# The order of one head's step, written anew on all five engines around row sums that run as column tiles of the TensorE array

## The reference, cut to what matters

```
q, k, v = silu(conv4(x @ W.T))                 # per head 128 wide, causal, 4 taps
q = scale**2 * rms(q); k = scale * rms(k)      # needs sum(q*q), sum(k*k) over the head
g = -exp(A_log) * softplus(x @ Wfa.T @ Wfb.T + dt_bias)
beta = sigmoid(x @ Wb.T)
for each token t:                              # S is 128 x 128 per batch and head
    S = S * exp(g_t)
    S = S + k_t * (beta_t * (v_t - k_t @ S))
    o_t = q_t @ S
out = rms(o) * o_norm_w * sigmoid(gate)
x = x + out @ Wo.T
x = x + experts(layernorm(x))
```

## Time and profile before

| what | value |
|---|---|
| median of 3 runs | 5112.28 us (5112.07 to 5114.02) |
| the profiled execution's own time | 5110.11 us |
| its span, first to last instruction | 5108.4 us |
| granted TensorE clock, mean | 0.988 |
| busy: PE / DVE / ACT / POOL | 93% / 73% / 66% / 56% |
| attention part, about | 0 to 4300 us |
| expert part, about | 4300 to 5108 us |

### The profile page before, as it was taken

One profiled execution on the slowest core, in us unless ns is written; L12 is line 12 of the kernel. 1 busy time (PEld: TensorE's weight loads), 2 busy tenths in 40 slices (PEclk: granted clock), 3 DMA queues, 4 the chain that ended last, 5 costly groups with the idle time before them and its releaser, 6 DMA issues.

```text
span 5108.4 us, 111671 instructions
## 1 busy us (share of the span) xinstructions
PE 4746.5 (93%) x28928; PEld 3617.8 (71%) x28928; DVE 3750.8 (73%) x8897; ACT 3347.4 (66%) x7216; POOL 2884.6 (56%) x6210
## 2 busy tenths in 40 slices
PE   6999999999999999999999999999999997999999
PEld 3777777777777777777777777777777775555555
DVE  5878777777777777777787777777777773555555
ACT  5777777777777777777777777777777772111111
POOL 4766666666666666666666666767676671000000
PEclk8999999999999999999999999999999998999999
DMA  2211111111111111111111111111111111000000
GB/s 82 62 36 37 37 37 37 33 36 35 37 35 36 37 37 37 32 37 35 37 35 37 37 37 37 37 33 37 35 37 35 37 28 35 13 8 12 8 12 13
DMA packets 214012, 173.09 MB, mean 34 GB/s; under 512 B 146272, under 2 KB 163936, under 8 KB 213216
## 3 DMA queue, kind: packets, MB, share of 16 engines
q1 hardware_dynamic: 213344, 165.49, 11.4%
HBM read 119.03 MB, written 46.40 MB: 32 GB/s over the span
## 4 chain that ended last, share of the span: by engine, by line
PE 64%; ACT 19%; issue 11%; POOL 2%; DVE 2%; DMA 1%; ACTq 0%; POOLq 0%; SPq 0%; DVEq 0%
PE bank L1589 10%; PE bank L1380 9%; PE bank L1281 8%; PE bank L1428 5%; PE bank L1402 4%; PE bank L1358 4%; PE bank L1599 4%; ACT L638 3%; ACT lx L574 3%; PE bank L1333 2%; PE bank L1433 2%; PE bank L1289 2%; PE bank L1415 2%; ACT T L584 2%; ACT e_sb L634 2%
## 5 line engine op out<-in xcount | busy, mean ns | idle before, releaser
L1380 PE MATMUL bank<-kq,kl 128*128 128x128 f32 x6144 | 853.3, 282 | 47.5 <-DVE kq L879 39.9
L387 POOL TENSOR_TENSOR kl<-kl,tot 128x256 f32<-128x256 f32 x768 | 507.1, 660 | 588.5 <-PE bank L1380 588.4
L1380 PEld LDWEIGHTS bank<-kq,kl 128*128 128x128 f32 x6144 | 750.0, 191 | 108.0 <-issue 70.1
L1281 PE MATMUL bank<-xT,par 128*128 128x512 f32 x1536 | 760.4, 605 | 0.4 <-ACT bexp L531 0.4
L406 POOL TENSOR_TENSOR mul<-pm,rm 32x14 f32<-32x14 f32 (+6 forms) x1792 | 528.4, 295 | 123.4 <-issue 23.0
L410 POOL TENSOR_TENSOR rm<-rm,mul 32x14 f32<-32x14 f32 (+6 forms) x1792 | 511.8, 286 | 142.3 <-POOL mul L406 2.4
L879 DVE TENSOR_TENSOR kq<-kq,tot 128x512 f32<-128x512 f32 x768 | 536.6, 699 | 0.0
L889 DVE COPY_PREDICATED AT<-mask,bank 128x256 f32<-128x256 uint32 x896 | 468.3, 523 | 0.0
L367 POOL TENSOR_TENSOR rstd<-rstd,minus_half 128x4 f32<-128x4 f32 x32 | 32.2, 1007 | 737.6 <-DVE rstd L824 737.6
L797 ACT ACTIVATE q<-bank 128x512 f32<-128x512 f32 x144 | 86.1, 598 | 521.4 <-PE bank L1589 521.4
L1402 PE MATMUL bank<-T,lx 128*128 128x64 f32 x3072 | 386.3, 269 | 3.8 <-issue 3.8
(11 more groups left out here) (176 smaller groups left out, 12512.9 us busy)
## 6 DMA issues: line engine op xcount, KB each, us to landing
par<-params_dram SPq DMA_DIRECT2D x128, 519.0 KB, 3.4
blocks_out<-lx SPq DMA_DIRECT2D x128, 256.0 KB, 2.0
lx<-blocks_in SPq DMA_DIRECT2D x128, 256.0 KB, 2.7
pm<-blocks_out SPq DMA_DIRECT2D x512, 8.0 KB
blocks_in<-rm SPq DMA_DIRECT2D x512, 8.0 KB
out_dram<-xall SPq DMA_DIRECT2D x16, 512.0 KB, 2.9
xall<-x_dram SPq DMA_DIRECT2D x5, 1536.0 KB, 7.1
lx<-ffn_dram SPq DMA_DIRECT2D x1, 3456.0 KB, 10.8
```

Of the source, the lines that this page charges most:

```text
L387: pool.tensor_tensor(halves(kl[:, :], w)[:, :, 0, :], src, totr.broadcast_to([P, SEQ // (2 * w), w]), ALU.mult).then_inc(s["kl_ready"], 1)
L1281: ins = pe.matmul(bank[t][:, :], par[p][:, at:at + P], chunk(xT, kt, SEQ), start=kt == 0, stop=kt == KT - 1)
L1380: ins = pe.matmul(dst[:, :, n], chunk(left, n), right[:, :, n, :, 1, :], start=True, stop=True)
```

## The change

Only the lists of calls at the end of each `step` are changed; the functions, the waits within them, the buffers and the arithmetic stay. Every engine has the same calls in a step as before. The whole diff, with 16 columns of indentation and the empty lines left out:

```diff
@@ -296,8 +296,6 @@
     sp.wait_ge(s["low_in"], 16 * NCH * (iB + 1))
     sp.sem_inc(s["sp_go"], 1)
-if B:
-    next_params()
 if D:
     blocks_from_pool()
     diagonals_back()
@@ -305,6 +303,8 @@
     low_levels_out()
     blocks_to_pool()
 next_x()
+if B:
+    next_params()
 supersteps(sp, lambda bn, first: None, step)
 sp.wait_ge(s["x_mm"], HIGH * NHEAD)
@@ -458,10 +458,10 @@
 if D:
     eliminate(iD, 10)
+    eliminate(iD, 11)
 if B:
     kl_update(0)
 if D:
-    eliminate(iD, 11)
     eliminate(iD, 12)
     eliminate(iD, 13)
     eliminate(iD, 14)
@@ -473,18 +473,13 @@
     softplus_high()
 if B:
     kl_update(3)
+    kl_update(4)
 if A:
     totals(1)
     totals(2)
     totals(3)
     totals(4)
-if B:
-    kl_update(4)
-if A:
     totals(5)
-    totals(6)
-    totals(7)
-next_rstd()
 if B:
     kl_update(5)
 if C:
@@ -496,11 +491,19 @@
 if B:
     eliminate(iB, 1)
     eliminate(iB, 2)
+if A:
+    totals(6)
+if B:
+    eliminate(iB, 3)
     kl_update(6)
-    eliminate(iB, 3)
+next_rstd()
+if B:
     eliminate(iB, 4)
     eliminate(iB, 5)
     eliminate(iB, 6)
+if A:
+    totals(7)
+if B:
     eliminate(iB, 7)
     eliminate(iB, 8)
     eliminate(iB, 9)
@@ -707,62 +710,64 @@
     after(act, s["su_mm"], 3 * (i - LAG + 1))
     act.activation(kT[pB][:, :], b_x[:, 0:3 * P], ACT.Copy).then_inc(s["kt_ev"], 1)
+if C:
+    w_evict(0)
+if A:
+    tap0(0, "q_mm")
 if B:
     k_copy()
-if C:
-    w_evict(0)
-if A:
-    tap0(0, "q_mm")
+if A:
+    tap0(1, "k_mm")
 if C:
     w_evict(1)
 if A:
-    tap0(1, "k_mm")
     softplus_exp()
     softplus_max()
     softplus_ln()
+if C:
+    w_evict(2)
+if A:
     tap0(2, "v_mm")
-if C:
-    w_evict(2)
 if D:
     t16_scale()
-if B:
-    lt16_scale()
-if A:
-    decay()
 if N:
     turned_x(nb, 0)
+if B:
+    lt16_scale()
 if D:
     tt16_evict()
-if C:
-    w_evict(3)
-if D:
     x_evict(4)
 if N:
     turned_x(nb, 1)
+if C:
+    w_evict(3)
+if A:
+    decay()
+if N:
+    fa_evict(nb)
+if C:
+    output_squares()
 if A:
     silu(0)
     silu(1)
-if C:
-    output_squares()
-if N:
-    fa_evict(nb)
 if D:
     tt_evict(4)
     x_evict(5)
 if A:
     silu(2)
     square(0)
+if B:
+    turned_v()
+if A:
+    square(1)
 if N:
     ga_evict(nb)
-if B:
-    turned_v()
-if A:
-    square(1)
 if D:
     tt_evict(5)
+if C:
+    turned_og()
+if D:
     x_evict(6)
-if C:
-    turned_og()
 if A:
     gate()
 if N:
@@ -1022,85 +1027,85 @@
     l_evict(0)
     kq_update(0)
     qk_evict(0)
+if A:
+    conv(0, 1)
 if C:
     s_update(0)
 if A:
-    conv(0, 1)
+    conv(0, 2)
 if C:
     residual(1)
 if A:
-    conv(0, 2)
     conv(0, 3)
+    conv(1, 1)
 if B:
     l_evict(1)
     qk_evict(1)
-if A:
-    conv(1, 1)
 if C:
     s_update(1)
 if B:
     kq_update(1)
 if A:
     softplus_one()
+if C:
+    residual(2)
+if A:
     softplus_rest()
 if B:
     l_evict(2)
-if C:
-    residual(2)
-if B:
+    qk_evict(2)
     kq_update(2)
-    qk_evict(2)
 if A:
     conv(1, 2)
     conv(1, 3)
 if B:
     l_evict(3)
+    qk_evict(3)
 if C:
     s_update(2)
 if B:
-    qk_evict(3)
+    kq_update(3)
+if C:
+    residual(3)
 if A:
     conv(2, 1)
-if B:
-    kq_update(3)
-if C:
-    residual(3)
-next_moments()
+    conv(2, 2)
+    conv(2, 3)
 if B:
     l_evict(4)
     qk_evict(4)
     kq_update(4)
-if A:
-    conv(2, 2)
 if D:
     t_update(4)
+if B:
+    l_evict(5)
+if C:
+    output_moments()
+if B:
+    kq_update(5)
 if A:
     kq_init(1)
-    conv(2, 3)
-if B:
-    l_evict(5)
-if C:
-    output_moments()
-if B:
-    kq_update(5)
+if B:
     qk_evict(5)
+if C:
+    outputs()
 if D:
     t_update(5)
-if C:
-    outputs()
 if B:
     l_evict(6)
+next_moments()
+if B:
     kq_update(6)
 if A:
     kq_init(0)
 next_scale()
-if D:
-    t_update(6)
 if B:
     qk_evict(6)
 if C:
     residual_stream(0)
     residual_stream(1)
+if D:
+    t_update(6)
 if A:
     scales()
     diagonal()
@@ -1468,26 +1473,26 @@
     pe.matmul(b_s[:, P:2 * P], chunk(TT[pB], n), R if n else chunk(vs[pB], 0),
               start=True, stop=True).then_inc(s["z_mm"], 1)
+if B:
+    level(0)
 if C:
     solve(0)
-if B:
-    level(0)
 if A:
     project(0, 0)
     project(0, 1)
+    project(1, 0)
 if C:
     state_update(0)
 if A:
-    project(1, 0)
+    project(1, 1)
 if C:
     k_times_s(1)
+if B:
+    level(1)
+if C:
     chunk_outputs(0)
-if B:
-    level(1)
-if C:
     solve(1)
 if A:
-    project(1, 1)
     project_f()
 if C:
     state_update(1)
@@ -1497,66 +1502,69 @@
     level(2)
 if A:
     project(2, 0)
+if C:
+    solve(2)
+if A:
     project(2, 1)
-if C:
-    solve(2)
 if B:
     level(3)
 if C:
     state_update(2)
+if N:
+    turn_next_x(nb, 0)
 if A:
     project_g(0)
     project_g(1)
     project_g(2)
-    project_g(3)
-if C:
+if C:
+    chunk_outputs(2)
     k_times_s(3)
 if D:
+    turn_16()
     lt_times_t(4)
 if N:
-    turn_next_x(nb, 0)
-if D:
-    turn_16()
+    turn_next_x(nb, 1)
+if C:
+    solve(3)
 if B:
     level(4)
-if C:
-    chunk_outputs(2)
-    solve(3)
 if N:
-    turn_next_x(nb, 1)
+    next_fa(nb)
 if C:
     state_update(3)
     chunk_outputs(3)
 if D:
     t_products(4)
-if N:
-    next_fa(nb)
 if B:
     level(5)
 if D:
     turn_t(4)
     lt_times_t(5)
+if A:
+    project_g(3)
+if B:
+    turn_v()
 if N:
     next_ga(nb)
 if D:
     t_products(5)
 if B:
-    turn_v()
     level(6)
 if D:
     turn_t(5)
+if C:
+    turn_og()
+if D:
     lt_times_t(6)
-if C:
-    turn_og()
 if N:
     next_beta(nb)
 if A:
     sums()
-if D:
-    t_products(6)
 if C:
     project_out(0)
     project_out(1)
+if D:
+    t_products(6)
 if A:
     turn_sums()
 if B:
```

32 lines of the change are left out of this document (16 added, 16 removed).

## The result

The changed kernel takes 5069.98 us (median of 4 runs, 5069.19 to 5071.58), the kernel before, run beside it on the same chip, 5113.15 us. The ratio is 0.9916, 95% interval [0.9901, 0.9931]: 43 us faster, where 85 were forecast. The profiled execution took 5070.19 us with a span of 5068.5 us.

A forecast was written before the change was run, and what follows sets the result against it. A ring through PE, DVE and a nearly full ACT bounds each step. Terms of -0.71, +0.05 and -0.02 give -0.68 us, times 125 is -85 us: 5027 us, forecast range 5000 to 5050, 8 in 10 within 4975 to 5095.

The forecast's parts named there:

- The ring: Step's chain: PE's first calls, q's convolution, project_f, ACT to square of k, sums, next step; other waits closed give only its gain.
- The ACT term: ACT, softplus to square of k: PE about 1.1 us sooner, so both idle gaps close, 0.71 us a step.
- rival C: POOL takes the bound: elimination steps stretched by DVE, 0.80 us each; one gives 5112 us, two 5215; chance 0.11.
- The start: DVE, step's start: s_update(0) behind q's first conv delays q's last taps some 0.2 us, mostly covered; 0.05 us charged.
- The step's sum: Ordinary step: all terms together -0.68 us, 31.6 to 30.9.
- small overlaps on ACT: ACT within the step: a further gain of 0.02 us a step.
- The POOL term: POOL, step's start: kl_update(0) written 4.9 us into the step, level(1) needs it at about 5.0; room 0.1 us.
- SP at nothing: SP's queue: next_params goes from first call to last, with 5 us of room left; costs nothing.
- The N and loop steps at -0.7: Head 7's step with extra matmuls and the step behind the loop's branch: each taken to gain 0.7 us.
- Rival B: Half the gain: unseen 0.1 to 0.2 us waits at level(1), turn_16 and level(5); 0.34 us a step, 5070; chance 0.20.
- Rival A: More comes back: PE's whole 1.1 us at level(5) reaches the step's end, 4975 us; chance 0.10.

The follow-up runs named there:

- 3: Changed kernel with s_update(0) put back ahead of the first tap of q on DVE, residual(1) behind that tap; 5118.1 us, ratio 1.0019.
- 5: Changed kernel with POOL's totals(1) held until level 4's eviction of kq, totals(4) to (6) moved down among the elimination's steps; 5042.11 us.
- 9: Changed kernel with totals(1) held back, later totals spread, kl_update(0) first on POOL, and the step's start on PE and DVE put back; 4979.19 us.
- 12: Changed kernel with POOL's totals(1) held until level 4's eviction on DVE is done, nothing else moved; 5084.54 us, ratio 0.9961.
- 11: Changed kernel with only the step's start put back as before on PE and DVE (state_update(0), s_update(0), residual(1)); 5055.59 us, ratio 0.9894.
- 4: Changed kernel with kl_update(0) as POOL's first call, ahead of elimination steps 10 and 11; 5064.75 us, ratio 0.9905.
- 10: Changed kernel with next_params put back at the front of SP's queue; 5076.45 us, ratio 0.9942.

## Why the prediction was half right

*The ring* held. In 3 some 0.5 us ahead of `project_f` became 0.5 us a step, in 5 and 9 what was taken out of it came off the step.

*The ACT term, "0.25 and 0.46 both close: 0.71 us a step", is the step that failed.* The mechanism was right and the size wrong: softplus to square went from 19.47 to 18.98 on average, 0.49 instead of 0.71. The premise was "PE reaches `turn_t(4)` and `lt_times_t(5)` about 1.1 us sooner". Counted from the softplus, it reaches them 0.5 us sooner: `level(5)`, right in front of them, starts 12.61 us behind the softplus before and 12.09 in the changed kernel. In 5, without the stretch, it is 11.65, and that is 0.96 sooner, near the 1.1. I had written that `level(5)` then waits for DVE, and took the middle of 0.8 and 1.4 without asking how long DVE's update would last at its new place. It lasts 1.12 us and not 0.69, since POOL's `totals(1)` begins 0.04 us ahead of it. In 5 and 12 the stretch is gone and so is the gap. I had used this very contention, but only for POOL's elimination, as rival C; the same pair of rows had to be asked in the other direction too. The Trainium skill ("SBUF — State Buffer", section "Who interferes with whom") says that a DVE instruction with two SBUF inputs contends with a GpSimd instruction that reads SBUF. The trace agrees (0.69, 1.12, and 0.68 with the neighbour held back); the prediction had quoted it and not applied it here.

With the stretch gone the term is even larger than forecast, 19.47 to 18.56 or 0.9 us. The bracket of 0.29 ahead of `x_evict(5)` cost more than it shows: between the starts of the two evictions lie 0.67 us with it and 0.33 without it [2407.52 to 2408.19, and 2413.72 to 2414.05 in 9], so 0.34.

*The start, "I charge 0.05 us to the ring".* First and last piece went from 12.08 to 12.21 in the mean, +0.13, and putting `s_update(0)` and `state_update(0)` back gave 0.22 in the changed kernel, so the rest of the new start gained 0.1. The path was another one than I had named. I had let the last tap of q eat up 0.23 us of room ahead of `project_f`. But in 3, where `project_f` does wait for that tap, it starts 0.05 us behind its end, so the room was 0.18 in the step that I read and 0.02 in the next one, where `project_f` started 0.07 behind. And in the changed kernel `project_f` starts some 0.24 us behind the last tap in most steps: the tap doesn't bind it. What is late is `level(1)`, 5.10 or 5.24 us behind `level(0)`, against 5.01 in 11. It stands behind `k_times_s(1)`, which reads `s_update(0)`; and that is late by `project(1, 0)`, now ahead of `state_update(0)` on PE, as well as by DVE's order. In the changed kernel 0.5 us of idle stand ahead of the first convolution, so DVE isn't short of time there, only in the wrong order.

*The step's sum.* -0.49 + 0.13 is -0.36, which is what heads 1 to 4 measured. Forecast was -0.68. Of the 0.32 between them the ACT term has 0.22, the start 0.08, and 0.02 were the "small overlaps on ACT", of which nothing is seen. Head 0's step, behind the N step, gained 0.72: its first and last piece had been 12.45 us and is 12.27 now, nearly like the others'. In the kernel before, DVE made the next batch's beta in that step (0.28 and 0.36 us, L840 and L842) ahead of `s_update(0)`, and PE waited for it:

```profile
2384.42 0.49 PE L1457 MATMUL bank<-lx,kq 128*128 128x128 f32 x2 [0.15 <-DVE lx L924]
```

`level(1)` started 4.57 us behind `level(0)` there and 4.15 in the other steps. In the changed kernel it is 5.25, as in the steps of heads 2 and 4: the idle time that now lies ahead of the first convolution takes these 0.6 us in. I had counted head 0's step as an ordinary one.

*The POOL term, "room of 0.1 us", and rival C.* `level(1)` has its kl in time in seven steps of eight. In head 6's it waits 0.26 us, and 4 shows the price, 0.48 us in that step, some 7 us in all. So C was true in one step of eight. It wasn't an elimination that was stretched but `next_rstd`, which my walk had left out, and `inverse_norms`, by 0.38 and 0.44 us, of which I had allowed for neither.

*SP at nothing* held within 6 us (10). *The N and loop steps at -0.7* came out at -0.31 and -0.20. The N step without a dip is 35.41, which is -0.97; the dips give two thirds of it back on average. The mean granted clock of the profiled executions went from 0.988 to 0.986; by that the dips cost the changed kernel some 10 us more than the one before (an estimate, 0.002 of the span).

*Rival B* gave the measured time, 5070, and two of the three places it named: `level(5)` (0.4 longer than in 5) and, in one step, `level(1)`. It had taken them for many small waits; they were one stretched instruction, the start, and one step. That its number came out is luck in good part. *Rival A*, 4975, isn't what this order does; the variant of 9 comes to 4979 by closing ACT's gap and the start, in ordinary steps of 30.6.

What stays open: what decides in which N steps the clock dips (below).

## What to carry to other kernels

When a list of calls is reordered, ask of every moved instruction not only when it starts but who reads SBUF beside it at the new place, on both engines: here a neighbour 0.04 us too soon made a 0.69 us update take 1.12, and without it (5) ordinary steps gain twice as much. A wait closed on one engine is worth what the ring around all of them gives, and the moves that close it may be a loss in part (5472 and 5278 us for one and two of them, 5165 for all but ACT's, against 5070 for all and 5110 for none). Price a move at the start of a step by undoing all engines' share of it together, since undoing one (3) makes a wait that neither kernel has.
